# A three-layer decoder block: cross-attention's value pieces and output rows an iteration later, LoRA rank parts stacked

## What is computed

```python
x = x + attn(layernorm(x))                      # 32 heads of 16
q = layernorm(x) @ Wq -> 32 heads of 128; k, v = ctx @ Wk, ctx @ Wv -> 8 heads of 128
q, k = rotary(q), rotary(k)
a = softmax(where(mask == 0, -1e9, q k^T / sqrt(128)))
x = x + (a v) @ Wo                              # Wo is 4096 x 512
A, B = lora_A, lora_B picked per group of 256 tokens (8 groups, rank 32), plus a shared pair
x = x + layernorm(x) @ W + bias + (y A^T) B^T + (y As^T) Bs^T      # y = layernorm(x)
```

## Time and profile before

| | |
|---|---|
| median of 3 runs | 1425.12 us (1423.65 to 1425.51) |
| the profiled execution's own time | 1423.42 us |
| its span, first to last instruction | 1421.6 us |
| busy: PE, PEld, DVE, ACT, POOL | 1389.5, 1151.6, 1021.8, 437.6, 530.1 us |
| longest wait of all: POOL for DVE's `rb` | 325.3 us in 97 times |
| mean granted TensorE clock | 0.996 |

### The profile page before, as it was taken

How to read it: one execution, slowest core, us unless ns; L and a number is a source line. 1 busy time by engine, 2 the same in 40 slices (tenths; PEclk the granted TensorE clock), 3 DMA queues, 4 the chain that set the end, 5 groups by cost and what they waited for, 6 DMA issues and landing times.

```text
span 1421.6 us, 27933 instructions
## 1 busy us (share of the span) xinstructions
PE 1389.5 (98%) x11600; PEld 1151.6 (81%) x11600; DVE 1021.8 (72%) x1470; ACT 437.6 (31%) x741; POOL 530.1 (37%) x459
## 2 busy tenths in 40 slices
PE   8999999999997799999999999999999999999999
PEld 6888888788886588888888888888888888888787
DVE  4755553888889877777777768768768768778753
ACT  5311233656656432122122122122122122121421
POOL 5422210444434525345344344344344344342231
PEclk9999999999999899999999999999999999999999
DMA  8653320000005011011011011012011011003011
GB/s 267 223 185 134 111 74 1 17 10 18 10 3 164 16 45 60 16 46 60 16 45 60 16 46 59 16 46 60 16 46 60 16 46 60 16 16 116 1 59 59
DMA packets 78859, 83.03 MB, mean 58 GB/s; under 512 B 9824, under 2 KB 50928, under 8 KB 78480
## 3 DMA queue, kind: packets, MB, share of 16 engines
q1 hardware_dynamic: 68832, 63.16, 14.1%
q10 hardware_dynamic: 9360, 17.04, 3.8%
q0 software_dynamic: 544, 1.06, 0.3%
HBM read 58.17 MB, written 23.07 MB: 57 GB/s over the span
## 4 chain that ended last, share of the span: by engine, by line
PE 61%; DVE 2%; POOL 1%; issue 1%; ACT 0%; ACTq 0%
PE p_ps_y L1272 6%; PE p_ps_y L1274 6%; PE p_ps_y L1273 6%; PE p_ps_s L1233 4%; PE p_ps_qk L75 4%; PE p_ps_qk L77 4%; PE p_ps_qk L76 4%; PE p_ps_s L1244 2%; PE p_ps_o L75 2%; PE p_ps_s L1274 2%; PE p_ps_s L1273 2%; PE p_ps_s L1272 2%; PE p_ps_o L76 2%; PE p_ps_o L77 2%; PE p_ps_s L75 2%; PE p_ps_s L77 2%
## 5 line engine op out<-in xcount | busy, mean ns | idle before, releaser
L1651 POOL TENSOR_TENSOR p_q_rot<-p_q_rot,p_rb 128x512 f32<-128x512 f32 x128 | 167.3, 1307 | 325.3 <-DVE p_rb L171 325.3
L1272 PE MATMUL p_ps_y<-p_wo_hi,p_o_hi 128*128 128x512 f32 x384 | 151.2, 394 | 1.9 <-DVE p_o_lo L1526 1.3
L1274 PE MATMUL p_ps_y<-p_wo_hi,p_o_lo 128*128 128x512 f32 x384 | 149.5, 389 | 0.0
L1273 PE MATMUL p_ps_y<-p_wo_lo,p_o_hi 128*128 128x512 f32 x384 | 149.5, 389 | 0.0
L75 PE MATMUL p_ps_qk<-p_xt_hi,p_wq_hi 128*128 128x512 f32 x312 | 129.9, 416 | 1.1 <-DVE p_xt_lo L1550 1.0
L1031 POOL TENSOR_TENSOR p_pn<-p_p,p_inv 128x512 f32<-128x512 f32 x64 | 66.1, 1064 | 153.4 <-DVE p_inv L920 151.2
L77 PE MATMUL p_ps_qk<-p_xt_hi,p_wq_lo 128*128 128x512 f32 x312 | 122.6, 393 | 0.0
L76 PE MATMUL p_ps_qk<-p_xt_lo,p_wq_hi 128*128 128x512 f32 x312 | 121.6, 390 | 0.0
L1380 ACT ACTIVATE p_pt_hi<-p_ps_s 128x512 fp32r<-128x512 f32 x64 | 38.2, 599 | 255.4 <-PE p_ps_s L1244 255.4
L1535 DVE TENSOR_TENSOR x_sb<-p_ps_y,x_sb 128x512 f32<-128x512 f32 x96 | 66.3, 691 | 68.0 <-PE p_ps_y L1274 67.0
L1386 ACT ACTIVATE p_o_hi<-p_ps_s 128x512 fp32r<-128x512 f32 x64 | 34.8, 595 | 232.2 <-PE p_ps_s L1259 232.2
(11 more groups left out here) (270 smaller groups left out, 3793.9 us busy)
## 6 DMA issues: line engine op xcount, KB each, us to landing
k_scratch<-p_k_out SPq DMA_DIRECT2D x32, 256.0 KB, 2.1
p_raw<-in_wq SPq DMA_DIRECT2D x32, 256.0 KB, 3.1
p_raw<-in_wo SPq DMA_DIRECT2D x32, 256.0 KB, 2.6
p_k_t<-k_scratch ACTq DMA_DIRECT2D x32, 256.0 KB, 2.6
p_v_in<-v_scratch ACTq DMA_DIRECT2D x32, 256.0 KB, 2.8
v_scratch<-p_v_out SPq DMA_DIRECT2D x24, 256.0 KB, 2.7
x_sb<-in_x SPq DMA_DIRECT2D x16, 256.0 KB, 2.9
out<-p_y SPq DMA_DIRECT2D x16, 256.0 KB, 2.0
```

The lines of the kernel that those rows point to most:

```text
L1272: nc.tensor.matmul(ps_y[t][:, :], oh, w_hi["o"][h][:, :], start=(h == 0), stop=False)
L1273: nc.tensor.matmul(ps_y[t][:, :], oh, w_lo["o"][h][:, :], start=False, stop=False)
L1274: mm = nc.tensor.matmul(ps_y[t][:, :], ol, w_hi["o"][h][:, :], start=False, stop=(h == H - 1))
L1651: nc.gpsimd.tensor_tensor(q_rot[:, h, :], q_rot[:, h, :], rb[:, :], ALU.add).then_inc(q_added, 1)
```

## The change

In the cross-attention `mix` and `output` run one loop body later than before, behind the next block's transposes; the two halves of `turn` stand together between `mix` and `scores`, and write to the banks `ps_free_q` and `ps_free_y`, not to the scores' banks. The loop is now for `it` = 0 to 30. POOL's and ACT's splits of `Wo` go to the second block of a group (b == 1) and those of group 0, with `values_lo(0)`, into the first loop body. In the LoRA layer `a_parts` holds hi and lo weights side by side in 128 columns, so that one matmul gives the rank rows of both, and `r_parts` and `b_hi` are stacked likewise: 8 matmuls instead of 12 for the ranks and 2 instead of 3 for a tile's rank rows; DVE adds the two halves in one more operation.

```diff
-        ps_p = ps_s
+        ps_p = [ps_free_q, ps_free_y]
@@ tensor
                 if h == 0:
                     need(pe, q_terms, (it - 1) * H + 3)
+                    need(pe, pt_ready, 2 * (it - 2) + 1)
...
-                need(pe, pt_ready, 2 * it)
+                need(pe, s_bound, 2 * it)
...
                 need(pe, pt_ready, 2 * it + half + 1)
-                need(pe, all_lo, 3 * TPB)
-                need(pe, q_terms, min((it + 1) * H + 2 * half + 2, ITS * H))
+                need(pe, all_lo, TILES)
+                need(pe, q_terms, min((it + 2) * H + 2 * half + 2, ITS * H))
...
-                turn(0, 0)
                 turn_tile(11)
-                turn(0, 1)
-                for it in range(LAST - 1):
-                    mix(it, 0)
-                    mix(it, 1)
+                for it in range(LAST):
+                    if it > 0:
+                        mix(it - 1, 0)
+                        mix(it - 1, 1)
+                    turn(it, 0)
+                    turn(it, 1)
                     scores(it + 1)
                     queries(it + 2, 0)
-                    output(it, 0)
+                    if it > 0:
+                        output(it - 1, 0)
                     queries(it + 2, 1)
-                    output(it, 1)
-                    turn(it + 1, 0)
+                    if it > 0:
+                        output(it - 1, 1)
+                    if it == LAST - 1:
+                        lin.combine_a(pe)
                     queries(it + 2, 2)
-                    turn(it + 1, 1)
-                    queries(it + 2, 3)
                     if it == 0:
                         turn_tile(12)
-                    output(it, 2)
-                    if it == 0:
                         turn_tile(13)
-                    output(it, 3)
+                    queries(it + 2, 3)
                     if it == 0:
                         turn_tile(14)
                         turn_tile(15)
+                    if it > 0:
+                        output(it - 1, 2)
+                        output(it - 1, 3)
                 mix(LAST - 1, 0)
                 mix(LAST - 1, 1)
-                scores(LAST)
...
@@ gpsimd
                 for h in range(H):
                     add_terms(0, h)
-                for h in range(H):
-                    split_o_lo(pool, 0, h)
-                values_lo(0)
...
                 for it in range(LAST):
                     g, b = it // NB, it % NB
-                    if b == 0 and g > 0:
+                    if b == 1 and g > 0:
                         for h in range(H):
                             split_o_lo(pool, g, h)
-                    values_lo(it + 1)
+                    if it > 0:
+                        values_lo(it)
                     add_terms(it + 2, 0)
                     normalise_p(it + 1, 0)
                     normalise_p(it + 1, 1)
+                    for h in range(1, H):
+                        if it == 0:
+                            split_o_lo(pool, 0, h - 1)
+                        add_terms(it + 2, h)
+                    if it == 0:
+                        split_o_lo(pool, 0, H - 1)
+                        values_lo(0)
...
@@ LoraLinear
-        product3(self.nc, self.ps_r[:, 0:self.GTOK], [(self.a_hi[:, c, :], self.a_lo[:, c, :], self.t_hi[q][:, c, :], self.t_lo[q][:, c, :])
-                                                      for c in range(KC)]).then_inc(self.r_done, 1)
+        for c in range(KC):
+            self.nc.tensor.matmul(self.ps_r[:, 0:self.GTOK], self.a_parts[:, c, :], self.t_hi[q][:, c, :], start=(c == 0), stop=False)
+            mm = self.nc.tensor.matmul(self.ps_r[:, 0:self.GTOK], self.a_parts[:, c, :], self.t_lo[q][:, c, :], start=False, stop=(c == KC - 1))
+        mm.then_inc(self.r_done, 1)
...
-            self.nc.tensor.matmul(self.ps_y[u][:, :], self.r_hi[:, tile], bh, start=False, stop=False)
-            self.nc.tensor.matmul(self.ps_y[u][:, :], self.r_hi[:, tile], bl, start=False, stop=False)
-            self.nc.tensor.matmul(self.ps_y[u][:, :], self.r_lo[:, tile], bh, start=False, stop=True).then_inc(self.y_done, 1)
+            self.nc.tensor.matmul(self.ps_y[u][:, :], self.r_parts[:, tile], self.b_hi[q][:, :], start=False, stop=False)
+            self.nc.tensor.matmul(self.ps_y[u][:, :], self.r_parts[:, tile], self.b_lo[q][:, :], start=False, stop=True).then_inc(self.y_done, 1)
...
-        self.nc.vector.tensor_tensor(self.r_lo[:, :], self.ps_r[:, 0:self.GTOK], self.r_hi[:, :], ALU.subtract).then_inc(self.rank_lo, 1)
+        self.nc.vector.tensor_tensor(self.r_rest[2 * RANK:4 * RANK, :], self.ps_r[0:2 * RANK, 0:self.GTOK], self.r_parts[0:2 * RANK, :],
+                                     ALU.subtract).then_inc(self.rank_lo, 1)
...
+        self.nc.vector.tensor_tensor(self.r_parts[2 * RANK:4 * RANK, :], self.ps_r[2 * RANK:4 * RANK, 0:self.GTOK],
+                                     self.r_rest[2 * RANK:4 * RANK, :], ALU.add).then_inc(self.rank_lo, 1)
```

More of the change, by code:

```diff
@@ L1782, in zero_b @@
         self.dead(pool)
-        for part in (*self.b_hi, *self.b_lo):
+        for part in self.b_lo:
             self.nc.gpsimd.memset(part[:, :].bitcast(F32), 0.0).then_inc(self.zeroed, 1)
@@ L1828, in tile_parts_hi @@
         need(act, self.b_back, LB - NPC)
-        self.nc.scalar.activation(self.b_hi[q][0:RANK, :], self.b_raw[:, n, :], ACT.Copy).then_inc(self.bg_hi, 1)
+        for first in (0, 2 * RANK):
+            self.nc.scalar.activation(self.b_hi[q][first:first + RANK, :], self.b_raw[:, n, :], ACT.Copy).then_inc(self.bg_hi, 1)
     def rank_parts_hi(self, act, n):
```

177 lines of the change are left out of this document (82 added, 95 removed).

## The result

The changed kernel takes 1429.2 us (median, 1428.03 to 1431.36), the kernel before on the same chip 1424.95 us (1423.65 to 1426.05): a ratio of 1.0031, 95% interval 1.002 to 1.0042. The forecast was 1428.0 us, with a chance of 0.42 for slower and 0.47 for no difference.

The account below looks back on a forecast made before the run. PE's own instruction stream was taken as the bound in the steady loop. Terms -7.4 - 1.0 + 0 + 8.4 + 2.9 + 0 = +2.9 us, plus 1.7 to the median, gave 1428.0 us; own range 1426.5 to 1429.5, wider range 1423.3 to 1430.8.

Parts of the forecast that it names:

- LoRA layer: LoRA layer: rank products go from 12 to 8 matmuls and sixteen tiles lose one matmul each, -7.4 us.
- transposes in one burst: Steady loop: eight transposes together cost 0.96 instead of 1.00 us in each of 29 iterations, -1.0 us.
- group boundary: Once a group: output rows' wait for POOL's weight split goes, an equal wait of `queries(., 0)` for `pt_lo` comes, 0.
- start, without the clock: First loop body: PE idles about 8 us until POOL's `v_lo` at 520.4; with work left over, +8.4 us.
- second stretch of low clock: After PE's second wait at the start: 6.9 us at 1.2 GHz do the work of 4.0, +2.9 us.
- end: Last output rows: the 1.30 us wait for `o_lo` goes, a 1.3 us wait for the last `pt_lo` comes, 0.
- work left over: Behind the last scores: four bursts of output rows (4 by 2.71) and one block's value pieces (1.7), 12.5 us.
- cover of 2.6 us: LoRA layer: DVE's added operation on a rank part, 0.45 us, fits in 2.6 us before the result's first use.
- third rival: Faster: step from transposes to scores costs 0.11, not 0.20, and the clock dip is absent; 1422.5 to 1419.0 us; chance 0.12.
- first rival: Start: the second clock dip is short or absent, sum 0 to +1.5, 1425.1 to 1426.6 us; chance 0.25.
- second rival: Start: low clock outlasts scores(2) into block 3's projections, 1.6 us more, sum +4.5, 1429.6 us; chance 0.20.

Follow-up runs that it names:

- first four others: Kernel before with stacked LoRA parts alone (0.9955); changed kernel with splits ahead of the loop (1.0007), second idle time filled (1.0025), both idle times filled (1.0024).

## Why the prediction came true, and where its terms were off

| term | predicted | measured |
|---|---|---|
| LoRA layer | -7.4 | -7.4 |
| transposes in one burst | -1.0 | +1.4 |
| group boundary | 0 (-3.5 to +3.5) | -1.3 |
| start, without the clock | +8.4 | +8.6 |
| second stretch of low clock | +2.9 (0 to +4.5) | +1.6 |
| end | 0 (-1.3 to +1.3) | +1.1 |
| sum | +2.9 | +4.0 |

The start and the end are told apart by the forecast's own 12.5 us of work left over (four bursts of output rows and one block's value pieces). The third score block comes 2.30 us sooner (53.17 instead of 55.47), so the start costs 12.5 - 2.3 = 10.2 us, of which 1.6 are the clock's. Behind the last scores it takes 6.23 more, which is 12.5 - 7.4 + 1.1.

**LoRA layer.** Right to 0.1 us, and shown by itself (942.50). The cover of 2.6 us held. What the forecast passed over is a single wait of 0.79 us of the first rank product for DVE's `a_parts`; it is part of the end term.

**Transposes in one burst.** This step failed, in its sign too. The forecast took 0.96 us from eight transposes that stood behind matmuls of their own shape and applied it behind value pieces, which use 64 rows of the array; it held that what those cost on leaving them stays. There the second transpose starts 0.055 us later, and the burst is 1.02 us. With one matmul put between, it is 0.97. Against it stands 1.00 in the forecast for the two short bursts of before. By the steps of a plain iteration they cost 0.99 (0.354 us each, and projections of 2.857 and 2.863 instead of 2.72 behind them), so the burst adds 0.03; the projection behind the scores takes 2.89 instead of 2.87 us, 0.02 more, and why is open. Together that is the step from 26.63 to 26.68 us between plain score blocks, +0.05 in each of 29, +1.4 us. The step from transposes to scores is 0.20, as taken; the third rival's 0.11 did not come.

**Group boundary.** The mechanism was named: `queries(., 0)` waits for `pt_lo` behind ACT's four copies. Its size is 0.20 us an occurrence (26.88 instead of 26.68), where the old wait cost 0.38 (27.01 instead of 26.63). I had put them equal; 7 by 0.18 is the 1.3 gained. Dividing ACT's splits takes away the other 1.4.

**The start.** Both halves of the working held. The scores of block 1 come 1.8 us earlier, as worked out (495.4 instead of 497.18). The value pieces were forecast for 520.4, 48.7 us after the first scores, and start 48.9 after them; their releaser is `v_lo`. Putting the splits ahead takes 3.45 us off. The rest of the loss is the work left over, four bursts of output rows and one block's value pieces; the steady loop does not win it back (775.10 against 774.98), and it stands behind the last scores.

**The clock.** The fall came, as the forecast has it, and the kernels with filled idle time show that the idle PE is its cause. The Trainium skill (TensorE: Matmul & The Clock Gate, "Why this matters for your kernels") warns of long gaps between bursts; here the clock fell behind a wait of 2.39 us already, shorter than the gaps that the page warns of. The price of the fall was taken too high: the forecast let the low clock last 6.9 us from the first value piece on, as in the first low stretch, and it lasted 3.7 (522.28 to 526.00). The anchor was wrong: both stretches are about as long (490.2 to 500.4 us before, 515.7 to 525.9 now), but the new one begins 6.6 us ahead of its first value piece and the old one 3.5, since the clock fell with the shorter wait already and not, as the forecast argued, because of the longer. That puts the cost at 1.6 instead of 2.9, just above the first rival's 0 to 1.5; the second rival, a low clock that outlasts the scores, did not come; whether the transposes helped to bring the clock back no run separates. Most of the low stretch (515 to 522 us) lay ahead of the value pieces, where POOL was the bound.

**The end.** The wait for the last `pt_lo` is 1.78 us, taken as 1.3; the `a_parts` wait of 0.79 was not seen; the wait for `pick` (0.8 us before) is gone. Together with the removed 1.30 that is +0.5; the other 0.6 is a remainder that no run tested; more changes between kinds of matmul may hold it. The bound of +1.3 held.

So the terms were off by +2.4, -1.3, +0.2, -1.3 and +1.1, in all +1.1 us from the first scores on. That the sum came out so near is luck in part: without their signs the errors are 6.3 us. The likelier of the two verdicts, no difference (0.47), did not come; the measured time lies 1.2 us above the forecast and within its own range of 1426.5 to 1429.5. The two profiled executions differ by 1.7 us more ahead of them (span +5.7), the medians by 4.25. That stretch was left untested; the first matmul of line 644, in a part that no kernel changed, already starts between 237.4 and 247.5 us in the profiles of the two kernels and of the first four others.

## What to carry to other kernels

Moving work one iteration later freed nothing in this loop, whose own stream is the bound (775.10 instead of 774.98 us); it only took that work from the first body, where another engine then has to keep up, and hung it behind the last. Ask first what the first body will wait for, and put preparations that are independent of the loop (weight splits here) ahead of it. A burst's price holds only behind the neighbour it was read beside. And before counting a shorter step on one engine as a gain, look at the next engine's list for what already stands ahead of its answer.

## What the runs showed of the hardware

- An idle PE can cost twice: the idle time, and the matmuls behind it at 1.2 instead of 2.4 GHz. Unused matmuls in the gap kept the granted clock at 1.00, and the value pieces and transposes behind it took 2.64 instead of 4.25 us.
- Behind a wait of 1.78 us that followed eight transposes the granted clock fell in one execution (4.00 us at 0.62), and behind 1.77 or 1.78 us at the same place in seven others it did not: 1.6 us between executions of the same stretch of code. Behind the waits of 2.33 to 2.39 us at 515 us it fell in all three profiles that have them.
- After a change of kind it is the second instruction that pays, beside the step into the new kind: 0.164 instead of 0.109 us for the second transpose behind value pieces, 0.34 instead of 0.23 us from the first 512-column matmul behind value pieces or scores to the next instruction. A change of shape is not needed for it: behind four transposes, on all 128 rows like the projection that follows, it is 0.32.
